# Products of constants that nobody reads, in TensorE's queue of a two-layer scan kernel

## The reference

```
x = x + L0(gn(x))     # RWKV: k, v, r projections, WKV recurrence forward and backward over 3136 positions,
                      # sigmoid(r) gate, layer norm over channels, output projection
x = x + L1(gn(x))     # Mamba: layer norm, in-projection, causal convolution of 4 taps, silu, x-projection,
                      # softplus step size, selective scan with 16 states, forward and backward, silu(z) gate,
                      # output projection
```

## Time and profile before

| | us |
|---|---|
| median of three runs | 20560.99 |
| the three runs | 20558.29 to 20561.16 |
| profiled execution | 20586.68 |
| its span, first to last instruction | 20584.9 |

### The profile page before, as it was taken

The page is one execution under the profiler, slowest core; times in us unless marked ns, Lnnn a source line. Parts: engine busy times, 40 slices in busy tenths (PEclk is TensorE's granted clock), DMA queues, the critical chain, the costliest instruction groups (busy, mean ns, idle before and its releaser), DMA issues. The chain is left out here.

```text
span 20584.9 us, 179901 instructions
## 1 busy us (share of the span) xinstructions
PE 17720.7 (86%) x43392; PEld 7706.0 (37%) x43392; DVE 17704.0 (86%) x14031; ACT 14006.9 (68%) x35077; POOL 17627.3 (86%) x10484
## 2 busy tenths in 40 slices
PE   7888988888888888888988888888898888888888
PEld 3433433334343343333433334333343333433334
DVE  7988979889798897988979789797997979979799
ACT  5757757577675776757767577676776757767577
POOL 6978969789797897979979799697997979979799
PEclk9989989899898998989989899898998989989899
DMA  2313313133131332313323133231332323323233
GB/s 83 132 63 126 134 73 132 63 127 134 73 132 63 126 134 74 131 63 126 134 75 131 63 129 129 75 131 66 132 123 75 132 73 131 118 74 132 70 133 119
DMA packets 528855, 2178.88 MB, mean 106 GB/s; under 512 B 96328, under 2 KB 243424, under 8 KB 527648
## 3 DMA queue, kind: packets, MB, share of 16 engines
q1 hardware_dynamic: 527648, 2165.99, 29.0%
HBM read 1905.47 MB, written 245.63 MB: 104 GB/s over the span
## 5 line engine op out<-in xcount | busy, mean ns | idle before, releaser
L1026 DVE TENSOR_TENSOR_SCAN arena<-ps,arena 128x897 f32<-128x897 f32 x5376 | 10977.2, 2064 | 1051.0 <-ACT arena L1182 718.4
L1234 POOL TENSOR_TENSOR arena<-arena 128x896 f32<-128x896 f32 x5376 | 9978.7, 1874 | 621.5 <-PE ps L956 524.0
L956 PE MATMUL ps<-arena,ident 128*128 128x448 f32 x21504 | 9142.6, 562 | 1141.1 <-POOL arena L1234 1141.0
L1166 ACT ACTIVATE ps<-arena,A 128x448 f32<-128x448 f32 x10752 | 6412.1, 632 | 2128.7 <-DVE arena L1026 2097.6
L956 PEld LDWEIGHTS ps<-arena,ident 128*128 128x128 f32 x21504 | 4050.3, 194 | 5882.2 <-issue 3545.5
L1226 POOL TENSOR_TENSOR arena<-arena 128x896 f32<-128x896 f32 x2240 | 4678.9, 2089 | 0.0
L1015 DVE TENSOR_TENSOR arena<-ps,arena 128x896 f32<-128x896 f32 x3136 | 3338.7, 1065 | 30.4 <-ACT ps L1128 30.4
L913 PE MATMUL ps<-arena,diag 128*128 128x448 f32 x5376 | 2199.3, 553 | 116.6 <-issue 114.6
L913 PEld LDWEIGHTS ps<-arena,diag 128*128 128x128 f32 x5376 | 1031.7, 194 | 1197.4 <-issue 1110.6
L1215 POOL TENSOR_TENSOR arena<-arena 128x448 f32<-128x448 f32 x672 | 758.4, 1137 | 455.4 <-DVE arena L995 455.4
L1182 ACT ACTIVATE arena<-arena 128x2 f32<-128x2 f32 x5376 | 1041.2, 194 | 53.3 <-DVE arena L1026 53.3
(11 more groups left out here) (160 smaller groups left out, 20216.6 us busy)
## 6 DMA issues: line engine op xcount, KB each, us to landing
arena<-bc_rows SPq DMA_DIRECT2D x1792, 896.0 KB, 5.1
x_projected<-arena SPq DMA_DIRECT2D x112, 672.0 KB, 3.5
y_forward<-arena SPq DMA_DIRECT2D x112, 672.0 KB, 3.6
arena<-x_projected SPq DMA_DIRECT2D x112, 672.0 KB, 7.7
arena<-y_forward SPq DMA_DIRECT2D x112, 672.0 KB, 4.1
x<-in_x SPq DMA_DIRECT2D x119, 336.0 KB, 3.6
x_normed<-arena SPq DMA_DIRECT2D x112, 336.0 KB, 2.8
arena<-x_normed SPq DMA_DIRECT2D x112, 336.0 KB, 4.2
```

Of the source, the lines that this page charges most:

```text
L956: m = e.matmul(y, ident[:, :], pr[:, q % NPR, a * T:a * T + T], start=False, stop=p == NP - 1 and a == 1)
L1026: e.tensor_tensor_scan(rev(hh[:, q % NH, 0:W2], s), rev(decays(q)[:, 0:W2], s), rev(bb[:, q % NB, 0:W2], s), car[:, k, n:n + 1] if i % NC ...
L1166: e.activation(two(decays(q))[:, a, :], dt[:, r % NDT, :], ACT.Exp, scale=Am[s][:, k, 2 * p + a:2 * p + a + 1]).then_inc(c_ex, 1)
L1234: e.tensor_tensor(pr[:, q % NPR, :].rearrange("p (a b) -> p a b", a=2), two(hh[:, q % NH, :]), cr[:, 2 * p:2 * p + 2, :], ALU.mult).then_i ...
```

## The change

TensorE gets further calls of `e.matmul`. Each takes the identity (`ident`) as weights and 384 columns of `skipd`, a constant, and writes a PSUM bank whose content nobody reads before the next product or copy that starts it anew. Nothing else is changed on any engine.

- Layer 0, `keys(u)` for u = 1 to 20: three calls into bank KB, behind the wait for `b_kv` and in front of the key product.
- Layer 0, behind all rounds: eight calls into bank 3, behind a wait until `b_xo` is 10, the update that is the last to read this bank.
- Layer 1, first chunk, into bank DUBANK: four behind the group norm's products, four behind `n1`, six behind `n2`, two behind the last `cv`, three behind `xp`.

That is 60 calls in layer 0's rounds, 8 behind them and 19 in layer 1, for each of the 16 images.

```diff
@@ -592,8 +592,15 @@
+        def busy(n, o):
+
+            for _ in range(n):
+                e.matmul(o, ident[:, :], skipd[:, 0, :, :].rearrange("p a b -> p (a b)"), start=True, stop=True)
+
         def keys(u):
             w.wait_ge(b_kv, u)
+            if u:
+                busy(3, ps[:, KB, 0:3 * 128])
             product(KB, 0, *divmod(u, 3)).then_inc(b_k, 1)
@@ -672,6 +679,8 @@
                 w.wait_ge(b_bv, U)
                 product(VB, 1, *divmod(U, 3)).then_inc(b_v, 1)
             side(U)
+        w.wait_ge(b_xo, nth(4, 1) + 1)
+        busy(8, ps[:, 3, 0:3 * 128])
@@ -871,6 +880,15 @@
         steps = Steps(plan_pe)
+
+        def busy(n):
+
+            for _ in range(n):
+                e.matmul(ps[:, DUBANK, 0:3 * 128], ident[:, :], skipd[:, 0, :, :].rearrange("p a b -> p (a b)"),
+                         start=True, stop=True)
+
+
+        behind = {("n1", 0): 4, ("n2", 0): 6, ("cv", 2): 2, ("xp", 0): 3}
@@ -937,7 +955,10 @@
                     m.then_inc(c_wt, 1)
-
+                if not i:
+                    busy(behind.get((name, k), 0))
+
+        busy(4)
         side(-10)
```

## The result

The changed kernel is slower. Over four runs each, it takes 20708.54 us (20707.06 to 20713.61) against 20561.08 us (20558.29 to 20573.37): ratio 1.007, interval 1.0057 to 1.0082. Its profiled execution took 20708.51 us, in the middle of its runs; that of before lay some 26 us above the median of its own.

The account below looks back on a forecast made before the run. No engine bounds it everywhere; VectorE bounds the early rounds, TensorE close behind. Loop and first scan +7.3, handover -2.7, so +4.6 us an image, +74 over 16: 20635 us on the median 20561, range 20480 to 20740.

Parts of the forecast that it names:

- Early rounds: Layer 0's loop, twelve intervals between L570 scans: TensorE becomes the bound, 79.8 us against 72.3 in the third image.
- The first interval: Between the first two L570 scans of layer 0's loop: 6.7 us with dummies at full clock, 8.3 before.
- the first scan: First L570 scan of layer 0: dummies ahead of it make it 1.0 us later, between 0.4 and 3.85.
- Late rounds: Layer 0's loop, last stretch of L570 scans: 2 us gained, 59.5 us against 61.5 in the third image.
- The walk: Late rounds, along TensorE's order from round 14's key product: last key product ends at +42.5 to +46.9, now +50.4.
- Handover: End of layer 0 to layer 1's first scan: eight calls cost +1.65 us, the whole gives -2.7 us an image.
- The step from the profiled execution to the median: Whole kernel: profile 25.7 us above the runs' median, so 20661 us on the profile became 20635 on the median.
- The rival that said faster: Whole kernel: dummies fit into idle time, clock fully given back; -3.7 us an image, 20502 us; chance 0.22.
- That the clock doesn't rise: Rival: late half stays at low clock, each triple costs 3.85 us; +29 us an image, 21030 us; chance 0.04.
- That the cases cancel: Rival: late rounds at 57 us and a free start leave +1.1 us an image, 20579 us; chance 0.22.

Follow-up runs that it names:

- one_per_unit: The changed kernel with one dummy call in place of three ahead of the key product in each unit; 20567.57 us, ratio to before 1.0001.
- late_only: The kernel before plus three dummy calls ahead of the key product in units 14 to 20 alone; 20582.54 us, ratio to before 1.0011.
- early_only: The kernel before plus three dummy calls ahead of the key product in units 1 to 13 alone; 20729.21 us, ratio to before 1.0078.
- chain_only: The kernel before plus only the nineteen dummies in layer 1's first chain, without the eight or the units' calls; 20527.78 us, ratio 0.9980.

## Why the prediction was right, and where it was not

It said slower, 20635 us and a range to 20740; it is 20708.54. The mechanism was right in the early rounds, which make up most of the cost; of the whole, 74 us were forecast and 147 came.

**Early rounds: right.** 79.8 us was worked out for twelve rounds, 81.0 measured, and a further call adds the forecast 0.64 a round. TensorE has taken VectorE's place as the bound. The first interval is 6.80 for 6.7, the first scan 0.85 later for 1.0. One premise beside it was wrong and did no harm here: VectorE's busy time of 5.65 us was taken for its round, which takes 5.81 at full clock without dummies and 6.0 with one call (one_per_unit).

**Late rounds: the step that failed.** The walk ended in 59.5 us, the measured mean is 62.3. The 2 us of gain were taken off the third image's 61.5, a loop of the long kind, and the sum was then compared with a mean in which the late rounds take 59.70. So against the mean of before the late rounds were to give nearly nothing, and cost 2.6. TensorE's timeline in the late rounds of the changed kernel, cut to the steps of the walk (L598 the dummies, L631 and L636 the L624 and L629 of before, L654 and L658 the output step):

```profile
2732.43 1.67 PE L587 MATMUL ps<-x,arena 96*128 96x448 f32 x4
2736.91 1.02 PE L631 MATMUL ps<-arena,ones 128*128 128x448 f32 x2 [2.81 <-ACT arena L709]
...
2740.46 2.90 PE L598 MATMUL ps<-skipd,ident 128*128 128x384 f32 x6
...
2759.45 0.99 PE L654 MATMUL ps<-arena,wo 128*96 128x448 f32 x2 [0.75 <-DVE arena L525]
...
2764.05 0.99 PE L654 MATMUL ps<-arena,wo 128*96 128x448 f32 x2 [1.03 <-DVE x L529]
...
2776.46 1.87 PE L636 MATMUL ps<-arena,ones 64*128 64x448 f32 x4 [3.85 <-POOL arena L769]
2778.25 4.21 PE L598 MATMUL ps<-skipd,ident 128*128 128x384 f32 x6
...
2784.26 1.77 PE L589 MATMUL ps<-x,arena 96*128 96x448 f32 x4
```

The walk starts where the key product ends, at 2734.1, and put L629 at +37.9 and the end of the last key product at +42.5 to +46.9. L636 came at +42.4, and the last key product ended at 2784.2, +50.1, where before it was +50.4. The 4.5 us by which L636 is late were missing from the walk. Behind the first wait (2.81 us) the clock fell for a while, so that the value product took 2.6 us for 1.65 and the first triple 2.74 for 1.95 (2.90 by its row); before the output steps TensorE now waits for VectorE's L525 and L529 (0.75 and 1.03); the rest is in smaller pieces. The last triple then ran at the low clock (4.21), right behind a wait for GpSimd that dummies in front of the wait did nothing to fill; this the walk had allowed for, in the upper end of its range. ScalarE feels all of it, as before with 9.08 us:

```profile
2784.38 0.55 ACT L693 ACTIVATE arena<-ps 128x448 f32<-128x448 f32 x1 [11.67 <-PE ps L592]
```

Here stood the 1.9 to 3.85 us of dummies on the one path that matters, between the closing's product and the key product. late_only shows the price alone.

**Handover: right in kind.** The eight calls put L333 2.06 us behind the end of VectorE's L574 (before 0.30), +1.76 where +1.65 was said; the handover gained 3.6 us where 2.7 were said.

**The step from the profiled execution to the median: wrong.** The profile of before was 25.7 us above its median and I subtracted this from the forecast. The changed kernel's profile is at its median. The excess belongs to before, whose images fall in and out of the low clock and differ from each other by up to 14 us in the loop; with TensorE always busy in the early rounds they differ by 2.4, and the runs lie within 6.6 us. So of the 73 us that the forecast missed, some 26 are this and 48 are 3.0 us an image: 2.8 in the late rounds and 1.2 in the early ones, less 0.9 in the handover.

**The rival that said faster** paid the dummies from idle time and the clock's return in full. early_only refutes the first half: a round goes from 6.05 to 6.75 us, above the 6.2 below which this rival had to keep it, so idle time and the clock's return together cover only 1.2 of a triple's 1.93 us. late_only refutes the second: the clock at 0.92 brings no shorter late stretch.

**The other two rivals.** That the clock doesn't rise is out, with 0.66 to 0.92 in the late rounds. That the cases cancel needed late rounds of 57 us; they take 62.3.

## What to carry to other kernels

Work added to keep a clock up must stand in a wait, not ahead of work that others wait for: 27 calls in the handover and ten in two late waits gained 0.48%, while 60 ahead of products lost 1.0%. Before adding it, set the engine's own work in a round beside the round's length; here 4.67 + 1.93 us against 5.65 foretold the early rounds within 1.5%. Room in the round doesn't make a call free: one a round cost at least 0.2 us of its 0.64. A wait at a block's end is shorter than it looks if the added work outlasts the other engines, as thirteen calls did by 2.8 us. A clock that is low beside waits for other engines is worth less than its share: price it from a walk along the order of the queue, including the dummies' own time at the low clock.

## What the runs showed of the hardware

The clock rose sooner behind dummies than behind products alone. In the third image of before, TensorE ran 96-row products back to back from 2620.91 on, and was at the low clock for another 13 us:

```profile
2620.91 3.35 PE L589 MATMUL ps<-x,arena 96*128 96x448 f32 x4
2624.05 3.19 PE L587 MATMUL ps<-x,arena 96*128 96x448 f32 x4
...
2630.36 3.35 PE L587 MATMUL ps<-x,arena 96*128 96x448 f32 x4
2633.51 2.04 PE L589 MATMUL ps<-x,arena 96*128 96x448 f32 x4
```

In the changed kernel three 128x128 dummies stand in front, and already the next product is at full clock:

```profile
2639.45 3.90 PE L598 MATMUL ps<-skipd,ident 128*128 128x384 f32 x6
2643.19 1.67 PE L589 MATMUL ps<-x,arena 96*128 96x448 f32 x4
```

The same place read in all 16 images, from the start of that product, or of the dummies in front of it, to the rise of the granted clock: before 3.7 to 6.1 us in five images and 13.2 to 16.5 in eleven; the changed kernel 2.9 to 6.2 in all sixteen, and one_per_unit, with a single call there, 3.3 to 6.0. That is why the first interval of before is now 4.86 us and now 8.3 or more, and the same in every image with dummies. In chain_only the clock rose behind four such calls, within their 5.00 us. Why products alone often took so much longer was not tried.
